# Routed expert results: from four accumulating tables to a plain row per token and rank, summed at the end

## What is computed

```python
scores = sigmoid(h @ gate_w.T)                       # 32 experts
# the best 4 of 8 groups, then the best 8 experts of each token
tki = top_k(masked, 8)
tkw = scores[tki] / sum * 2.5
g = silu(h @ w_gate[e]); u = h @ w_up[e]
routed[t] = sum over the 8 chosen e of  tkw[t, e] * (g * u) @ w_down[e]
x = x + routed + shared
```

## Time and profile before

| | us |
|---|---|
| median of 3 runs | 3751.42 (3747.28 to 3752.35) |
| the profiled execution | 3735.88 |
| its span, first to last instruction | 3734.1 |

### The profile page before, as it was taken

How to read it: one execution, slowest core, us unless ns; L and a number is a source line. 1 busy time by engine, 2 the same in 40 slices (tenths; PEclk the granted TensorE clock), 3 DMA queues, 4 the chain that set the end, 5 groups by cost and what they waited for, 6 DMA issues and landing times.

```text
span 3734.1 us, 62492 instructions
## 1 busy us (share of the span) xinstructions
PE 3381.2 (91%) x21744; PEld 1647.2 (44%) x21865; DVE 2410.8 (65%) x6369; ACT 1801.1 (48%) x3594; POOL 510.3 (14%) x450
## 2 busy tenths in 40 slices
PE   6999989999999989999999889999999889999991
PEld 2353445334362445344452445344452445347870
DVE  5568576755668576755768576855768566854542
ACT  2755444363755434453846434454836434544540
POOL 0000020000001120000002120000002020007885
PEclk9999999999999999999999999999999999999995
DMA  6313001305314101306214101215223201848997
GB/s 218 120 37 71 20 2 49 53 1 191 102 32 95 43 3 49 51 16 210 79 27 93 37 9 48 47 60 178 69 41 85 103 17 46 246 155 214 162 155 159
DMA packets 183739, 316.84 MB, mean 85 GB/s; under 512 B 29956, under 2 KB 138884, under 8 KB 178052
## 3 DMA queue, kind: packets, MB, share of 16 engines
q1 hardware_dynamic: 152360, 270.37, 25.8%
q0 software_dynamic: 29040, 39.86, 6.1%
q10 hardware_dynamic: 2032, 2.61, 0.2%
HBM read 176.41 MB, written 116.70 MB: 78 GB/s over the span
## 4 chain that ended last, share of the span: by engine, by line
PE 69%; DVE 19%; issue 4%; ACT 4%; DMA 2%; SPq 1%; POOL 1%; DVEq 0%; POOLq 0%; ACTq 0%
PE ps L608 8%; PE ps L591 7%; PE ps L430 5%; DVE mx L774 5%; PE ps L535 4%; PE ps L1910 4%; PE ps L1807 3%; PE ps L1848 3%; PE ps L596 3%; PE ps L487 2%; PE ps L1518 2%; PE ps L1831 2%; DVE ps L771 2%; PE ps L639 2%; PE ps L573 2%
## 5 line engine op out<-in xcount | busy, mean ns | idle before, releaser
L712 ACT ACTIVATE PT<-ps 128x512 f32<-128x512 f32 (+2 forms) x1280 | 644.0, 564 | 324.0 <-PE ps L596 125.8
L774 DVE TENSOR_REDUCE mx<-ps 128x1 f32<-128x512 f32 (+3 forms) x768 | 431.1, 618 | 77.2 <-PE ps L535 39.0
L591 PE MATMUL ps<-QS,KS 99*128 99x512 bf16 (+2 forms) x1280 | 418.6, 368 | 11.4 <-ACT PT L712 8.2
L535 PE MATMUL ps<-KS,QS 96*128 96x512 bf16 (+3 forms) x1280 | 391.7, 367 | 19.7 <-DVE mx L771 6.9
L771 DVE CUSTOM_DVE_ANT_0 ps<-ps,mneg 128x512 f32<-128x512 f32 x512 | 340.9, 718 | 82.0 <-PE ps L535 78.9
L608 PE MATMUL ps<-PT,VP 128*32 128x512 f32 (+3 forms) x2560 | 371.1, 573 | 0.0
L408 POOL TENSOR_TENSOR rstd<-mv,half 128x4 f32<-128x4 f32 x20 | 20.3, 1017 | 2477.8 <-DVE mv L375 2477.8
L430 PE MATMUL ps<-mneg,identb 128*128 128x512 bf16 x1087 | 289.0, 389 | 46.4 <-DVE a_fin L2041 15.4
L591 PEld LDWEIGHTS ps<-QS,KS 99*128 99x128 bf16 x1280 | 108.5, 97 | 390.1 <-ACT PT L712 236.4
L1498 POOL DMA_INDIRECT sums<-wbuf,ctxT x159 | 247.9, 1559 | 48.5 <-issue 37.5
L535 PEld LDWEIGHTS ps<-KS,QS 96*128 96x128 bf16 x1280 | 127.3, 100 | 226.2 <-DVE mx L774 75.8
(11 more groups left out here) (368 smaller groups left out, 5997.4 us busy)
## 6 DMA issues: line engine op xcount, KB each, us to landing
slot_rows<-in_padrows SPq DMA_DIRECT2D x32, 725.0 KB, 20.6
scores<-a_fin SPq DMA_DIRECT2D x64, 256.0 KB, 3.1
a_fin<-scores SPq DMA_DIRECT2D x32, 512.0 KB, 4.8
KS<-KP SPq DMA_DIRECT2D x240, 64.0 KB, 2.6
g_xb<-slot_rows SPq DMA_DIRECT2D x105, 145.0 KB
a_Y<-in_wA SPq DMA_DIRECT2D x4, 3072.0 KB, 12.8
scores<-a_fin SPq DMA_DIRECT2D x64, 192.0 KB, 2.9
a_fin<-scores SPq DMA_DIRECT2D x12, 1024.0 KB, 8.9
```

The lines of the kernel that those rows point to most:

```text
L535: last = nc.tensor.matmul(o, m["QS"][0:KR, h, i * P:(i + 1) * P], m["KS"][0:KR, h, f:f + w], start=True, stop=not c.causal)
L591: last = nc.tensor.matmul(o, m["KS"][0:KST, h, j * P:(j + 1) * P], m["QS"][0:KST, h, q0:S], start=True, stop=plain)
L712: nc.scalar.activation(m["PT"][:, mp % 2, j % 2, e, 0:w], ps[:, SLOTS + n % TURNED, 0:w], ACT.Exp, scale=HD ** -0.5).then_inc(g("exp"), 1)
L774: nc.vector.tensor_reduce(m["mx"][:, h % 2, i, f // BANK:f // BANK + 1], ps[:, k % SLOTS, 0:w], AX.X, ALU.max, negate=True).then_inc(g("sl ...
```

## The change

- The accumulating scatter goes. Every routed result row gets a row of its own in a DRAM table `parts`: token x 8 + rank of the expert among the token's eight. POOL's DMA for a block is a plain scatter (new line 1525), with no wait for earlier ones; the y ring of 24 places and VectorE's wait on it stay, now on 24 semaphores.
- `slot_rows` grows from 290 to 320 numbers a row: 256 features, 32 weights, 32 row numbers of `parts`, one for each expert. VectorE picks weight and row number by the block's expert.
- The row numbers are made by a new function `mark_parts` on POOL: nine operations that each wait for the one before, after `chosen` (and a small one ahead of it). `gate_slots` now waits for it (`parts_marked`).
- At the head of stage G POOL starts 7 of the last 32 `to_slot`, and the other 25 one after every second block.
- `zero_sums` is gone. The residual goes to `x_kept_rows`, and is loaded back in two DMAs of 1 MB into the place of two masks, by SP, ahead of block 65 and behind its wait for `scattered`.
- Padding rows are written in the same way, with longer rows, and 31 spare blocks of them instead of one.
- At the end `parts` (16.8 MB) comes back in eight pieces of 2.1 MB, in a ring of 6 places over the experts' weights. VectorE adds eight rows for each token in eight operations for a piece.

```diff
         def g_sp(sp):
...
             for b in range(NBLOCK):
                 if b == NFULL:
                     sp.wait_ge(scattered, 16 * B * NI * TOPK)
+                    for h, kept in enumerate(m["kept"]):
+                        sp.dma_start(kept, x_kept_rows[TOKENS // 2 * h:TOKENS // 2 * (h + 1), :].rearrange("(t p) d -> p t d", p=P)).then_inc(g("kept_in"), 16)
                 if b >= RX:
                     sp.wait_ge(g("y_up"), b - RX + 1)
...
-            for r in range(NACC):
-                sp.wait_ge(g(f"added{r}"), 16 * len(range(r, NBLOCK, NACC)))
-            for q in range(B):
-                for r in range(NACC):
-                    sp.dma_start(m["sum"][:, r, NI * q:NI * (q + 1), :], sums[r][S * q:S * (q + 1), :].rearrange("(t p) d -> p t d", p=P)).then_inc(g(f"sums_in{q}"), 16)
+            for r in range(RY):
+                sp.wait_ge(g(f"part_out{r}"), 16 * len(range(r, NBLOCK, RY)))
+            def parts_back(q):
+                if q >= RB:
+                    sp.wait_ge(g("summed"), q - RB + 1)
+                rows = TOKENS * TOPK // NB
+                sp.dma_start(m["back"][:, q % RB, :, :], parts[rows * q:rows * (q + 1), :].rearrange("(t p k) d -> p t (k d)", p=P, k=TOPK)).then_inc(g(f"parts_in{q}"), 16)
...
         def g_pool(pool):
             g = lambda s: sm["G", s]
-            for k in range(NI * TOPK):
+            for k in range(SLOTS_FIRST):
                 to_slot(k)
-            pool.wait_ge(x_stored, 16)
-            pool.wait_ge(zeroed, 16 * NACC)
             for b in range(NBLOCK):
+                if b % 2 == 0 and SLOTS_FIRST + b // 2 < NI * TOPK:
+                    to_slot(SLOTS_FIRST + b // 2)
                 pool.wait_ge(g("y_up"), b + 1)
-                if b >= NACC:
-                    pool.wait_ge(g(f"added{b % NACC}"), 16 * (b // NACC))
-                nc.gpsimd.indirect_dma_start(out=sums[b % NACC], out_offset=bass.IndirectOffsetOnAxis(ap=token[:, b % RY:b % RY + 1], axis=0),
-                                             in_=MG["y"][:, b % RY, :], in_offset=None, compute_op=ALU.add).then_inc(g(f"added{b % NACC}"), 16)
+                nc.gpsimd.indirect_dma_start(out=parts, out_offset=bass.IndirectOffsetOnAxis(ap=part_row[:, b % RY:b % RY + 1], axis=0),
+                                             in_=MG["y"][:, b % RY, :], in_offset=None).then_inc(g(f"part_out{b % RY}"), 16)
...
+        def mark_parts(pool, ch, m):
+            to = [m["upto"][:, r, :, :] for r in range(2)]
+            half_e = NE // 2
+            ch.link(nc.gpsimd.tensor_tensor(first_part[:, :], first_part[:, :], moeC[:, NE + 18 + NI:NE + 18 + 2 * NI], ALU.add))
+            pool.wait_ge(sm["F", "chosen"], 1)
+            ch.link(nc.gpsimd.memset(m["upto"][:, :, :, 0:half_e], 0.0))
+            ch.link(nc.gpsimd.tensor_copy(to[0][:, :, half_e:], m["rp"][:, :, :]))
+            for r, step in enumerate((1, 2, 4, 8, 16)):
+                a, b = to[r % 2], to[(r + 1) % 2]
+                ch.link(nc.gpsimd.tensor_tensor(b[:, :, half_e:], a[:, :, half_e:], a[:, :, half_e - step:half_e + NE - step], ALU.add))
+            ch.link(nc.gpsimd.tensor_tensor(b[:, :, half_e:], b[:, :, half_e:], m["rp"][:, :, :], ALU.subtract))
+            nc.gpsimd.tensor_tensor(xn[:, :, DM + NE:DM + 2 * NE], b[:, :, half_e:], spread(first_part[:, :], 2, [P, NI, NE]), ALU.add).then_inc(parts_marked, 1)
...
+            for q in range(NB):
+                rows = m["kept"][NT // NB * q // NK][:, NT // NB * q % NK:NT // NB * q % NK + NT // NB, :]
+                back = m["back"][:, q % RB, :, :].rearrange("p t (k c) -> p k t c", k=TOPK)
+                dve.wait_ge(g(f"parts_in{q}"), 16)
+                for k in range(TOPK // 2):
+                    last = nc.vector.tensor_tensor(back[:, k, :, :], back[:, k, :, :], back[:, k + 4, :, :], ALU.add)
+                ch.link(last)
+                for k in range(2):
+                    last = nc.vector.tensor_tensor(back[:, k, :, :], back[:, k, :, :], back[:, k + 2, :, :], ALU.add)
+                ch.link(last)
+                ch.link(nc.vector.tensor_tensor(back[:, 0, :, :], back[:, 0, :, :], back[:, 1, :, :], ALU.add))
+                nc.vector.tensor_tensor(rows, rows, back[:, 0, :, :], ALU.add).then_inc(g("summed"), 1)
```

More of the change, by code:

```diff
@@ L1434, in decoder @@
         moe_signals = ("tables", "late_in", *(f"x_in{r}" for r in range(RX)), "xt_mm", "xt_up", "gu_mm", "silu", "hid", "ht_mm", "ht_up", "y_mm", "y_up",
-                       *(f"added{r}" for r in range(NACC)), *(f"sums_in{q}" for q in range(B)), "summed")
-        sm.update({("G", signal): s for signal, s in zip(moe_signals, [s for (stage, _), s in list(sm.items()) if stage in "CE"])})
+                       *(f"part_out{r}" for r in range(RY)), "kept_in", *(f"parts_in{q}" for q in range(NB)), "summed")
+        sm.update({("G", signal): s for signal, s in zip(moe_signals, [s for (stage, _), s in list(sm.items()) if stage in "BCE"])})
         def x_block(b):
@@ L1449, in load_experts @@
                 sp.dma_start(MG["W"][:, e, :], io["wF"][NSH + e]).then_inc(sm["G", "late_in"] if e in LATE else experts_in, 16)
[L1451 to L1454 removed]
         def pad_experts(sp):
[L1458 removed]
+            sp.dma_start(slot_rows[NE * ROOM:NE * ROOM + NSPARE * P, :], io["padtail"]).then_inc(padded, 16)
             for e in range(NE):
@@ L1618, in g_dve @@
             nc.vector.tensor_scalar(table[:, 0, :], part, NE - 1.0, None, ALU.min)
-            nc.vector.tensor_scalar(table[:, 1, :], at, NE * ROOM / P, None, ALU.min).then_inc(g("tables"), 1)
+            nc.vector.tensor_scalar(table[:, 1, :], at, NE * ROOM / P + NSPARE - 1, None, ALU.min).then_inc(g("tables"), 1)
             dve.wait_ge(g("tables"), 1)
@@ L2086, in a_dve @@
             dve.wait_ge(g("bank_up"), len(A_BANKS))
-        GATE_SIGNALS = [sm["F", signal] for signal in ("lg_mm", "lg_exp", "chosen", "rank_mm", "gate_chain")] + [ranks_read]
+        GATE_SIGNALS = [sm["F", signal] for signal in ("lg_mm", "lg_exp", "chosen", "rank_mm", "gate_chain")] + [ranks_read, parts_marked]
         def ker_mem(sb2):
@@ L2268, in other_stages @@
                         load_weights(sp, ORDER[ORDER.index(s) + 1])
-                    if last and s == "C":
-                        zero_sums(sp)
                     if last and s == "E":
@@ L2305, in _ @@
                             next_pool(pool)
+                        else:
+                            mark_parts(pool, ch, MF)
                     else:
@@ L2310, in _ @@
                 if b < rounds - 1:
+                    ch = Chain(pool, pool_chain)
+                    mark_parts(pool, ch, MT)
                     st.end()
```

88 lines of the change are left out of this document (46 added, 42 removed).

## The result

| | us |
|---|---|
| before, median of 4 runs | 3751.38 (3747.28 to 3752.35) |
| after, median of 4 runs | 3780.51 (3776.49 to 3781.85) |
| ratio, with 95% interval | 1.0079 (1.0063 to 1.0095) |
| the profiled execution of after, its span | 3781.6, 3779.8 |

What follows compares the result with a forecast made beforehand. In stage G PE set the pace until POOL's adding scatters fell behind and held up the end. Tail start -38.7, tail +20.6, head 0 gave -18 us: median 3751.4 to 3733, range 3718 to 3745.

Steps and rivals of the forecast that it cites:

- POOL's pace: Stage G: a plain result scatter costs POOL 0.96 + 0.30 = 1.26 us instead of the adding one's 1.86.
- Rival 3: A POOL scatter costs 1.86 us whether it adds or not: slower, 3786 us; chance 0.07.
- So PE sets the pace throughout: Stage G: blocks stay 1.661 us apart; without a new wait the last result stands at 3647.3, 8.6 us earlier.
- rival 5: VectorE's picking by expert or busier HBM adds 0.1 us a block, 16 us: 3749, no change; chance 0.06.
- The stall at block 65: PE waits for block 65's rows behind late to_slot and residual loads: 9 us plus 1.5 of slow clock, 2 to 14.
- rival 2: No stall at block 65, as loads overlap or to_slot come sooner: 10.5 us less, 3722; chance 0.2.
- The head: Start of stage G: mark_parts makes gate_slots 2.4 us later, fewer early to_slot cancel it: 0, from -2 to +2.5.
- The credit for moving `to_slot` away from the head: Head of stage G: six to_slot, 0.9 MB or 2.4 us of transfer, come later, against the 2.4 us delay.
- The tail: Return of parts after the blocks: 54 us against 33.4, cost 20.6, at 5.25 us a piece of 2.1 MB.
- Rivals 1 and 4: Return of parts slower: 6.0 us a piece, 3738, chance 0.15; or q1's 240 GB/s, 8.7 a piece, 3760, chance 0.04.
- Stages A to F: Before stage G: stage A's wait is free, longer padding fits behind the old one, dropping zero_sums is worth nothing.
- The sum: Whole kernel: -38.7 (start of the tail) + 20.6 (tail) + 0 (head) = -18 us.

Runs made afterwards that it cites:

- g1: Changed kernel, unchanged, run again in a group where the kernel before takes about 3740 us: ratio 0.9961 to the kernel before.
- h1: Changed kernel, unchanged, run a third time, in a group where the kernel before takes about 3751 us: ratio 1.009 to the kernel before.
- g3: Changed kernel with stage G's signals on the old semaphores and both residual loads moved behind all block loads: 3718.8 us, ratio 0.994 to the kernel before.
- e3: Kernel before with the adding left out of its result scatters, plain writes into the four tables, sums not made: ratio 0.9876 to the kernel before.
- the early pick: Version of g3 with VectorE's copy of the row numbers moved ahead of its wait for PE's down product: ratio 1.0072 to the kernel before.
- g4: As g3, with all 32 to_slot at the head of stage G instead of 7: ratio 0.9943 to the kernel before.
- j1: Changed kernel with all 32 to_slot at the head of stage G, where the kernel before takes about 3751 us: ratio 1.0029 to it.

## Why the prediction was wrong, and where it was right

- **POOL's pace: right.** 0.962 + 0.30 us. Rival 3 is out: the same 0.96 us stands in the measured execution and in g1, so on both kinds.
- **"So PE sets the pace throughout": the step that failed.** It costed the 25 `to_slot` that move in between blocks by POOL's time alone (0.5 us a pair, taken up by the ring of 24) and let PE keep 1.661 us. In the group of the measurement the rows of DMAs that they make also hold SP and what PE signals, some 2 us for each `to_slot`. That is 49 us between h1 and g1, of the 57 by which h1's span (3778.9) is longer than g1's (3722.3). The rest is 5.5 us in blocks 62 to 99, among them the row at result 85, and 1.6 ahead of the last stage F. The trace of before didn't show it: by its time it came from kind 3740, where no profile has these gaps at every fourth block. There was a sign: the profiled execution lay 15 us under the three timed runs, which agreed within 5. I added the gap as a constant. It was a difference in kind.
- **The same step had a second, smaller error.** Even on kind 3740 the pace is 1.69 us (g3, blocks 66 to 158; 1.66 in the first 99 blocks before), 0.03 x 159 = 5 us. That is rival 5's mechanism at a third of its size. Plain scatters into four tables keep 1.66 (e3), so it isn't the plain scatter as such; the early pick may have given back 0.02 of it; whether the rest is the longer rows stays open.
- **The stall at block 65: right**, cause too. 7.9 us in g1 where 9 plus 1.5 were forecast, within 2 to 14; rival 2 is out. (In the measured execution PE waits 3.80 us for these rows.) PE turned block 65 at 3496.78, 6.52 us after it had come to it, where the earlier trace rows show 3485.44. Putting the loads elsewhere gave 5.5 us in the medians (g1 3724.3, g3 3718.8; the intervals of the two ratios overlap, but the 8 us are gone from the trace).
- **The head: right within its bounds, on kind 3740.** Counted from POOL's line 408 of the last F, `gate_slots` comes 1.5 us later than before (2.4 forecast), as `mark_parts` takes 4.1 us, not 5. The first result stands 48.8 to 51.1 us behind that line, before 48.6 to 49.0. So 0 to 2.5 us are lost. The credit for moving `to_slot` away from the head doesn't show: `gate_slots` to the first result takes 27.1 us in g3 and in g4, which has all 32 there.
- **The tail: right.** SP's first load to the end: 53.0 us (54 forecast), in g1 52.9, from this line to 3722.3:

```profile
3669.38 4.68 SPq L1504 DMA_DIRECT2D g_W<-parts  x6
```

  The first piece landed 7.7 us after it, as worked out, and a piece took VectorE 5.2 us, with gaps of at most 0.2. Rivals 1 and 4 are out: the pieces kept up with VectorE, and 2.1 MB each 5.2 us is 403 GB/s. For a load from HBM into SBUF the Trainium skill, "DMA: Bandwidth & Descriptors", "Where 436 GB/s comes from", gives a bound of about 358 GB/s for a core. This trace, with one core at work, doesn't agree.
- **Stages A to F** were rightly costed at nothing.
- **The sum.** On kind 3740 it was 3741.22 to 3724.31, 17 us, where it said 18. To hit it that closely was partly luck: in the two traces the start of the tail, counted from the last F, came 34.2 us earlier (38.7 forecast: the slower pace against a shorter stall), and the tail 19.5 longer (20.6), which is 15. The prediction named one number for a time that has two values, 3724 and 3781, and its chances (0.83 for faster) left nothing for a cost that this trace could not show.

## What to carry to other kernels

When the profiled execution lies well outside the spread of the timed runs, it may come from conditions that the timed runs didn't have: read its mechanisms, but don't take its waits as those of the timed runs, and keep a chance for costs that it can't show. Indirect DMAs started one right behind the other can cost more than their issuer's time. Where engines signal each other every microsecond, look how long such rows get and time them; the `to_slot` with pauses between them cost nothing here. And before two versions that each mend a loss are believed, run the lossy one beside them.

## What the runs showed of the hardware

- One program's time had two levels, 3740 and 3751 us, by group of runs, and the same edit was worth -0.4% on one and +0.8 to 0.9% on the other.
- On kind 3751, while POOL started indirect scatters of 128 rows 1.27 us apart, register instructions of SP took 0.7 us instead of 0.04, and ACT took up PE's work up to 19 us late (j1), with the DMA engines moving only 158 GB/s. A row of 32 `to_slot` did it, and so did a row of four result scatters of 1024 bytes a row (3.2 to 4.2 us to the next result instead of 1.64). `to_slot` started 1.47 us apart or more took no longer than on kind 3740.
- A plain indirect scatter costs POOL 0.96 us with rows of 1024, 1160 and 1280 bytes, the adding one 1.56, and each is followed by 0.30.
- The plain scatter in place of the adding one is worth 45 us by itself (e3, 3694 for 3739), before the return of twice the bytes takes 20 back: from the last result to the end e3 needs 37.3 us and g1 57.2.
